# A four-layer graph network on one core: edge sums by feature, two linear layers as one product, and the last layers with the output in groups of 512 nodes

## The reference, cut to what matters

```python
# L3, on nodes v = relu(layernorm(x)); all widths 128 except edge_attr and u (64)
msg = relu(concat(v[src], edge_attr) @ W1a + b1a)
msg = msg @ W1b + b1b
agg = mean of msg over the edges that end in a node (0 where there is none)
out = concat(v, agg, u[0]) @ W2a + b2a
out = relu(out) @ W2b + b2b
return x + out
```

## Time and profile before

| | |
|---|---|
| median of 3 runs | 9359.47 us (9359.37 to 9371.02) |
| profiled execution | span 9364.4 us; no separate device time is given for it, so its span stands 4.9 us above the median |
| TensorE busy | 7028.5 us, 75% |
| VectorE busy | 5660.6 us, 60% |
| ScalarE, GpSimd busy | 2515.7 us, 27%; 2656.2 us, 28% |
| near block of the edge pass | about 8963 to 9216 us of the span |
| the three `dense` calls | 9216.2 to 9350.0 us |
| output transfer | 9350.3 to the end at 9364.4 us |

### The profile page before, as it was taken

The page is one execution under the profiler, slowest core; times in us unless marked ns, Lnnn a source line. Parts: engine busy times, 40 slices in busy tenths (PEclk is TensorE's granted clock), DMA queues, the critical chain, the costliest instruction groups (busy, mean ns, idle before and its releaser), DMA issues. The chain is left out here.

```text
span 9364.4 us, 133857 instructions
## 1 busy us (share of the span) xinstructions
PE 7028.5 (75%) x35740; PEld 4596.9 (49%) x35792; DVE 5660.6 (60%) x16783; ACT 2515.7 (27%) x5863; POOL 2656.2 (28%) x2952
## 2 busy tenths in 40 slices
PE   4777777775566659940488699999998777777787
PEld 4555555453122224420477544444445666666676
DVE  6777777775589990059899800000014777777786
ACT  0222222222467740020388600000001333310001
POOL 0777777776470000000000000000002444444410
PEclk9767776766679989975799899999999999999998
DMA  3333333334975538849566478787886766642363
GB/s 99 103 103 105 105 104 103 105 105 167 393 231 164 168 114 306 299 195 426 205 215 216 144 262 276 262 287 256 295 284 200 181 180 179 179 111 63 63 178 88
DMA packets 969628, 1759.77 MB, mean 188 GB/s; under 512 B 102288, under 2 KB 665125, under 8 KB 905315
## 3 DMA queue, kind: packets, MB, share of 16 engines
q1 hardware_dynamic: 683820, 1335.73, 44.1%
q0 software_dynamic: 110720, 276.01, 9.0%
q10 hardware_dynamic: 174394, 139.51, 5.5%
HBM read 1412.04 MB, written 338.80 MB: 187 GB/s over the span
## 5 line engine op out<-in xcount | busy, mean ns | idle before, releaser
L768 POOL DMA_INDIRECT bucketed<-arena,wide x1563 | 1515.6, 970 | 726.5 <-issue 714.0
L1920 PE MATMUL psum<-wide,arena 128*128 x6496 | 1209.9, 329 | 400.5 <-DVE arena L1979 393.9
L1920 PEld LDWEIGHTS psum<-wide,arena 128*128 128x128 f32 x6496 | 989.9, 195 | 618.3 <-issue 493.3
L1787 POOL DMA_DIRECT2D table<-wide x13 | 9.7, 743 | 4316.2 <-DVE wide L1711 4316.2
L1979 DVE TENSOR_SCALAR arena<-wide,tile_first 128x128 f32 x3248 | 870.8, 300 | 472.3 <-PE psum L1920 293.8
L1841 POOL DMA_INDIRECT arena<-table,src_i x832 | 803.3, 966 | 1009.1 <-PE psum L1937 872.4
L1660 PE MATMUL psum<-arena,h 128*128 128x512 f32 (+1 forms) x2548 | 1048.6, 570 | 19.1 <-DMA arena<-adjacency 17.5
L922 PE MATMUL psum<-arena 128*128 128x512 bf16 x2253 | 695.7, 442 | 435.0 <-DVE arena L870 259.4
L665 PE MATMUL psum<-arena 128*113 128x177 bf16 x1568 | 534.4, 341 | 416.2 <-ACT wide L687 374.6
L870 DVE TENSOR_SCALAR arena<-sums 128x512 bf16<-128x512 int16 x2304 | 799.9, 347 | 0.0
L659 PE MATMUL psum<-w_edge,arena 128*128 128x256 f32 x1568 | 786.9, 597 | 0.0
(11 more groups left out here) (398 smaller groups left out, 11006.0 us busy)
## 6 DMA issues: line engine op xcount, KB each, us to landing
arena<-adjacency SPq DMA_DIRECT2D x294, 1024.0 KB
arena<-adjacency SPq DMA_DIRECT2D x98, 1568.0 KB, 7.8
adjacency<-wide SPq DMA_DIRECT2D x588, 256.0 KB
arena<-adjacency SPq DMA_DIRECT2D x196, 640.0 KB, 3.9
arena<-adjacency SPq DMA_DIRECT2D x147, 768.0 KB
arena<-bucketed POOLq DMA_DIRECT2D x208, 528.0 KB, 6.0
arena<-adjacency SPq DMA_DIRECT2D x49, 1792.0 KB, 6.9
arena<-adjacency SPq DMA_DIRECT2D x49, 1344.0 KB, 6.1
```

The source lines that it names most:

```text
L768: e.indirect_dma_start(bucketed, bass.IndirectOffsetOnAxis(ap=places[k][0:size, c:c + 1], axis=0), rows[k][0:size, c, :], None).then_inc(s ...
L1920: e.matmul(flat[:, ds((chunk & 3) * 512 + 2048, P)], lhsT=hot[:, i % 8, :], rhs=table_in[:, ds(tile * P, P)], start=False, stop=True, skip ...
```

## The change

It does five things.

1. In both blocks of the edge pass the operands of the matmul change places: the messages are now lhsT and the one-hot matrix rhs, so that the 128x128 sum comes out with features on the partitions, and `h` collects sums by feature. The first three lines of work of `dense` (scale, transpose, copy) fall away.
2. W1b @ `W["agg"]` is formed once, before `sage(1)`, by a `run` of nine steps; so are b1b @ `W["agg"]` (`agg_bias`) and the u part of b2a. One product with `w_agg` takes the place of the products with W1b and `W["agg"]`.
3. The node part, v @ `W["h"]` plus `agg_bias` where the node has any edge, is computed in `sage(3)`: 49 more products behind the old ones in `product`, and 49 `scalar_tensor_tensor` on VectorE (`kept_rows`), written over `sums`. `linear` and the passes wait for `kept_rows` now.
4. b2b is added to `x` by one GpSimd instruction over 128x6272 in the near block.
5. `tail()` takes the place of the three `dense` calls, the `run` and `store`: one block in which the 13 groups run through first product, scale and add (VectorE), transpose, bias and ReLU (ScalarE), second product, add to `x`, and each group's own output transfer.

Two of the row vectors loaded at the start become columns, and `dense`'s semaphores go; `gin_mlp` returns its semaphores for use in `tail`.

```diff
-        for name in ("L0_gnn_b1", "L0_gnn_b2", "L0_gnn_gamma", "L0_gnn_beta", "L2_gnn_b1", "L2_gnn_b2"):
+        for name in ("L0_gnn_b1", "L0_gnn_b2", "L0_gnn_gamma", "L0_gnn_beta", "L2_gnn_b1", "L2_gnn_b2", "L3_gnn_b1b", "L3_gnn_b2a"):
             col[name] = sb("c_" + name, [P, 1])
             loads.append((col[name][:, :], t[name].rearrange("(f a) -> f a", a=1)))
...
-                     "L3_gnn_b1a", "L3_gnn_b1b", "L3_gnn_b2a", "L3_gnn_b2b"):
+                     "L3_gnn_b1a", "L3_gnn_b2b"):
...
-        def turn(buffer, k):
...
-        def dense(inputs, finish, reader=0):
...
...
-
-        gin_mlp()
+            return [Baton(signal, GROUPS) for signal in (s_first, s_mid, s_second, s_feat, s_norm, s_turn, s_added)]
+
+        gin_signals = gin_mlp()
...
+        w_agg = W["L3_gnn_W1b"]
+        run([("tensor", lambda e, _: e.transpose(psum[:, 0, 0:P], W["L3_gnn_W1b"][:, :], ident[:, :]), 1),
+             ("vector", lambda e, _: e.tensor_copy(junk[:, :], psum[:, 0, 0:P]), 1),
+             ("tensor", lambda e, _: e.matmul(psum[:, 1, 0:D], lhsT=junk[:, :], rhs=W["agg"][:, :], start=True, stop=True), 1),
+             ("vector", lambda e, _: e.tensor_copy(junk[:, :], col["L3_gnn_b1b"][:, :].broadcast_to([P, P])), 1),
+             ("tensor", lambda e, _: e.matmul(psum[:, 2, 0:D], lhsT=junk[:, :], rhs=W["agg"][:, :], start=True, stop=True), 1),
+             ("tensor", lambda e, _: e.matmul(psum[:, 3, 0:1], lhsT=W["u"][:, :], rhs=u0[:, :], start=True, stop=True), 1),
+             ("vector", lambda e, _: e.tensor_copy(w_agg[:, :], psum[:, 1, 0:D]), 1),
+             ("vector", lambda e, _: e.tensor_copy(agg_bias[:, :], psum[:, 2, 0:D]), 1),
+             ("vector", lambda e, _: e.tensor_tensor(col["L3_gnn_b2a"][:, :], col["L3_gnn_b2a"][:, :], psum[:, 3, 0:1], ALU.add), 1)])
...
-                            e.wait_ge(s_node if more else s_added, g - 1 + (seen if more else 0))
+                            e.wait_ge(s_node if more else s_kept, g - 1 + (seen if more else 0))
...
+                        for c in range(n // P):
+                            last = e.matmul(psum[:, node_bank(p, k), c * P:(c + 1) * P], lhsT=part(wide, a + c * P, P), rhs=W["h"][:, :],
+                                            start=True, stop=True)
+                        last.then_inc(s_root, 1)
...
                                     e.wait_ge(s_row, after[p - 2])
+                                    e.wait_ge(s_kept, after[p - 2])
...
+                    def kept_rows(p, k):
+                        g = PASSES[p][0] + k
+                        a, n = dst_groups[g]
+                        e.wait_ge(s_root, g + 1)
+                        for c in range(n // P):
+                            t = a // P + c
+                            last = e.scalar_tensor_tensor(result[:, t * P:(t + 1) * P], agg_bias[:, :], s["some"][:, t:t + 1],
+                                                          psum[:, node_bank(p, k), c * P:(c + 1) * P], ALU.mult, ALU.add)
+                        last.then_inc(s_kept, 1)
...
                                     table_rows(p, k)
+                                    kept_rows(p, k)
                     if not more:
                         for k in range(PASSES[-1][1]):
                             table_rows(len(PASSES) - 1, k)
+                            kept_rows(len(PASSES) - 1, k)
 
...
-                            last = e.matmul(psum[:, n % 4, 0:D], lhsT=onehot[:, n % 4, c, :], rhs=ring[:, n % DEEP, c, :], start=c == 0, stop=c == PAIR - 1)
+                            last = e.matmul(psum[:, n % 4, 0:P], lhsT=ring[:, n % DEEP, c, :], rhs=onehot[:, n % 4, c, :], start=c == 0, stop=c == PAIR - 1)
...
+                @block.gpsimd
+                def _(e):
+                    e.tensor_tensor(x[:, :, :], x[:, :, :], row["L3_gnn_b2b"][:, :].unsqueeze(1).broadcast_to(tiles()), ALU.add).then_inc(s_biased, 1)
+                    e.wait_ge(s_biased, 1)
...
-                            last = e.matmul(psum[:, n % DEEP, 0:D], lhsT=near_hot[:, n % DEEP, c, :], rhs=near_in[:, g % DEEP, at:at + P],
+                            last = e.matmul(psum[:, n % DEEP, 0:P], lhsT=near_in[:, g % DEEP, at:at + P], rhs=near_hot[:, n % DEEP, c, :],
...
-        dense([(*mean_of_sums(), W["L3_gnn_W1b"])],
-              [("vector", lambda e, i, p: e.tensor_tensor(stage[1][:, :, :], row["L3_gnn_b1b"][:, :].unsqueeze(1).broadcast_to(tiles(BATCH)),
-                                                          s["some"][:, ds(i * BATCH, BATCH)].unsqueeze(2).broadcast_to(tiles(BATCH)), ALU.mult)),
-               ("vector", lambda e, i, p: e.tensor_tensor(batch(wide, i), stage[1][:, :, :], p, ALU.add))], reader=1)
-
-        run([("vector", lambda e, _: e.tensor_copy(junk[0:D_EDGE, :], u0[:, :].broadcast_to([D_EDGE, P])), 1),
-             ("tensor", lambda e, _: e.matmul(flat[:, 0:D], lhsT=junk[0:D_EDGE, :], rhs=W["u"][:, :], start=True, stop=True), 1),
-             ("vector", lambda e, _: e.tensor_tensor(row["L3_gnn_b2a"][:, :], row["L3_gnn_b2a"][:, :], flat[:, 0:D], ALU.add), 1)])
-        dense([(*nodes_of(nodes), W["h"]), ("vector", lambda e, i, out: e.tensor_copy(out[:, :, :], batch(wide, i)), W["agg"])],
-              [("vector", plus_row("L3_gnn_b2a", lambda i: batch(wide2, i))),
-               ("scalar", lambda e, i, p: e.activation(batch(wide2, i), batch(wide2, i), ACT.Relu))])
-        dense([(*nodes_of(wide2), W["L3_gnn_W2b"])],
-              [("vector", plus_row("L3_gnn_b2b", lambda i: batch(wide2, i))),
-               ("vector", lambda e, i, p: e.tensor_tensor(batch(x, i), batch(x, i), batch(wide2, i), ALU.add))])
-        s_out = sem("s_out")
-
-        def store(e, _):
-            e.dma_start(out[0:full_nodes * P, :].rearrange("(i p) f -> p i f", p=P), x[:, 0:full_nodes, :]).then_inc(s_out, 16)
-            e.dma_start(out[full_nodes * P:N_NODES, :], x[0:N_NODES - full_nodes * P, full_nodes, :]).then_inc(s_out, 16)
-            e.wait_ge(s_out, 32)
-            return e.nop()
-        run([("sync", store, 1)])
+        def tail():
+            hidden = [part(arena, 512 * k, 512) for k in range(2)]
+            summed, pre, flipped, hid, product, finished, stored = gin_signals
+            with nc.Block() as block:
+                @block.tensor
+                def _(e):
+                    def first(g):
+                        a, n = dst_groups[g]
+                        if g >= 2:
+                            e.wait_ge(pre.sem, pre.at + g - 1)
+                        for c in range(n // P):
+                            last = e.matmul(psum[:, g % 2, c * P:(c + 1) * P], lhsT=part(h, a + c * P, P), rhs=w_agg[:, :], start=True, stop=True)
+                        last.then_inc(summed.sem, 1)
+
+                    def flip(g):
+                        a, n = dst_groups[g]
+                        e.wait_ge(pre.sem, pre.at + g + 1)
+                        if g >= 2:
+                            e.wait_ge(hid.sem, hid.at + g - 1)
+                        for c in range(n // P):
+                            last = e.transpose(psum[:, 2 + g % 2, c * P:(c + 1) * P], part(sums, a + c * P, P), ident[:, :])
+                        last.then_inc(flipped.sem, 1)
+
+                    def second(g):
+                        a, n = dst_groups[g]
+                        e.wait_ge(hid.sem, hid.at + g + 1)
+                        if g >= 2:
+                            e.wait_ge(finished.sem, finished.at + g - 1)
+                        for c in range(n // P):
+                            last = e.matmul(psum[:, 4 + g % 2, c * P:(c + 1) * P], lhsT=hidden[g % 2][:, c * P:(c + 1) * P], rhs=W["L3_gnn_W2b"][:, :],
+                                            start=True, stop=True)
+                        last.then_inc(product.sem, 1)
+
+                    first(0)
+                    first(1)
+                    for g in range(GROUPS):
+                        flip(g)
+                        if g + 2 < GROUPS:
+                            first(g + 2)
+                        if g:
+                            second(g - 1)
+                    second(GROUPS - 1)
+
+                @block.vector
+                def _(e):
+                    def before_relu(g):
+                        a, n = dst_groups[g]
+                        e.wait_ge(summed.sem, summed.at + g + 1)
+                        for c in range(n // P):
+                            t = a // P + c
+                            last = e.scalar_tensor_tensor(part(sums, t * P, P), psum[:, g % 2, c * P:(c + 1) * P], s["rcount"][:, t:t + 1],
+                                                          part(sums, t * P, P), ALU.mult, ALU.add)
+                        last.then_inc(pre.sem, 1)
+
+                    before_relu(0)
+                    before_relu(1)
+                    for g, (a, n) in enumerate(dst_groups):
+                        if g + 2 < GROUPS:
+                            before_relu(g + 2)
```

(27 more changed lines are left out.)

72 lines of the change are left out of this document (5 added, 67 removed).

## The result

| | before | after |
|---|---|---|
| median of 4 runs each | 9362.70 us (9359.37 to 9371.02) | 9272.53 us (9265.40 to 9279.41) |
| span of the profiled execution | 9364.4 us | 9277.6 us |

The ratio is 0.9899, 95% interval 0.9887 to 0.9911: faster by 90.2 us in the medians, and by 86.8 us between the two profiled spans. Forecast were 9273 us and 9278.5 for the span.

A forecast was written before the change was run, and what follows sets the result against it. TensorE was taken to bound mid-sage(3), TensorE and VectorE the near block, hand-overs the dense calls. Terms -113.4 + 10.7 + 4.8 + 12 = -85.9 us gave a 9278.5 span, 9273 median; range 9257 to 9293.

The forecast's parts named there:

- tail for the `dense` calls and the output: End of the kernel: the new tail takes 35 us in place of 148.2, saving 113 us.
- `sage(3)`, its last three passes and its end: sage(3): 49 added node products lengthen it by 10.7 us (9 to 14).
- run of nine steps: Ahead of sage(1): nine dependent small steps that nothing covers, +4.8 us (3 to 7).
- GpSimd's add against VectorE: Near block: GpSimd's 14.1 us add holds up VectorE's one-hots, about 2 us covered; +12 us (0 to 14).
- operands swapped, loads: Edge matmuls in both blocks and the row loads made column loads: 0 us.
- The period: Tail: TensorE sets the pace at 2.24 us per full group, VectorE needing 1.7 us.
- start at half clock: Tail's beginning: the first 16 product instructions run at 0.22 instead of 0.112 us, costing 1.8 us.
- the clock rival: Tail: clock stays at half, 4.4 us a group, tail 60 us, whole 9298; chance 0.10 for any slower pace.
- Its rival: Tail's output: 13 transfers on one queue delay each other, some 10 of 14.4 us return, 9283; chance 0.06.
- passes 0 and 1: sage(3): products of 32 tiles fall into TensorE's saturated stretch and cost 7.2 us in full.
- pass 2: sage(3)'s last pass: 12 tiles (2.7 us) fall partly into TensorE's adjacency waits; 1.5 us taken, between 0.5 and 2.7.
- the last five tiles: End of sage(3): bare products and kept_rows delay the last table_rows and the next stage by 2 us.

The follow-up runs named there:

- b1: Changed kernel with each waited-for memory value passed through max(value, 0): 9345.46 us.
- b0: Kernel before the change with each waited-for memory value passed through max(value, 0): 9430.63 us.
- c1: b1 without the root product and kept_rows in sage(3), so the output lacks the node part: 9335.81 us.
- r0: Changed kernel with bounds asserted on each register value that a wait reads: 11582.8 us, near block 262.7 us.
- r1: r0 with GpSimd's add of b2b left out: 11575.0 us, near block 252.1 us.
- b3: b1 with the operands of both edge matmuls swapped back: 9345.09 us.
- b2: b1 with b2b added by VectorE in sage(3) instead of GpSimd and the nine-step run moved into sage(1)'s block: 9332.52 us.
- c2: b1 with all output transfers of the tail waiting for the last group: 9357.48 us, tail 44.7 us.
- c3: b1 with the tail's same instructions ordered one group behind the other, without interleaving: 9398.20 us, tail 88.6 us.
- r2: r0 with GpSimd's add replaced by two 128x6272 memsets that nobody reads: 11578.4 us, near block 250.9 us.
- c0: b1 with GpSimd adding b2b group by group in the tail instead of in the near block: 9337.67 us, tail 33.5 us.
- r3: r0 with b2b added by VectorE behind kept_rows in sage(3) instead of by GpSimd: 11559.4 us, near block 252.3 us.

## Why the prediction was right

| term | forecast | between the profiles |
|---|---|---|
| tail for the `dense` calls and the output | -113.4 | -114.7 |
| `sage(3)`, its last three passes and its end | +10.7 | +9.3 (b1 less b0 +9.9, b1 less c1 +9.6) |
| run of nine steps | +4.8 | +4.05 (4.55 in b1) |
| GpSimd's add against VectorE | +12 | +9.6 (r0 less r1 +10.6) |
| operands swapped, loads | 0 | 0 (b3) |
| stages ahead of `sage(1)` | not in the sum | +2.8 |
| `sage(1)`, `sage(2)`, first pass of `sage(3)`, start of the far block | not in the sum | +2.4 |
| what is left | | -0.25 |
| sum | -85.9 | -86.8 |

The two rows "not in the sum" are stretches in which the change alters nothing, and executions of one program differ in them by as much. The last copy before `sage(1)` ended at 5416.4 us in c1 and at 5423.6 in b1, which are the same up to that point, and `sage(1)` with `sage(2)` varied by 4.5 us.

So the mechanisms were right, term by term, but that the sum came out to 0.9 us is in part luck: all four terms that are not nothing were forecast too dear, by 0.75 to 2.4 us and 5.9 together, and 5.2 us from stretches that the forecast rightly left at nothing stand against them in this pair of executions. The median has its own luck. The forecast of 9273 starts from 9359.47 us, and the kernel before measured 9362.70 with the fourth run; the change was forecast at 85.9 us and is 90.2 in the medians.

*The tail.* The period was forecast at 2.24 us and is 2.22; TensorE sets it, as VectorE has 1.81 us (forecast 1.7; four `scalar_tensor_tensor` take 1.12 us with the last one's end, and 8 take 2.16, so one is 0.26 more, as forecast). The term that was mis-sized, and the only one that matters here, is the 1.8 us for a start at half clock. In the profiled execution the first 16 instructions took 2.02 us, at full clock. But the term is no invention: in b2 and c2 the same 16 took 3.29 and 3.57 us, with the clock at 0.60 over b2's first 3.8 us:

```profile
9296.43 3.29 PE L2039 MATMUL psum<-w_L_gnn_W1b,h 128*128 128x128 f32 x16 [1.75 <-PEq L1977]
```

The pause before them is 1.75 us in all of them. The term is paid in some executions, and then costs 1.1 us of the tail (b2: 34.4 for 33.3). The prediction's ground against the clock rival was read too well, though: it says that the clock rose within a few us of dense work. In that call the products still ran at half clock 6 us after the first slow ones, and at full clock 5 us later, with a pause of 1 us before each batch all the while:

```profile
9326.27 3.36 PE L1102 MATMUL psum<-w_L_gnn_W2b,arena 128*128 128x128 f32 x14 [1.00 <-ACT arena L1074]
...
9331.50 1.83 PE L1102 MATMUL psum<-w_L_gnn_W2b,arena 128*128 128x128 f32 x14 [0.99 <-ACT arena L1074]
```

That all groups ran at full clock was no small matter: c3, the same instructions in another order, ran at half clock to its end, so the clock rival (a tail of 60 us) was not far off. What the two traces show side by side is that TensorE is busy 28.0 of 33.5 us with the interleaved order, waiting for 0.33 us at the longest once it has begun, and 60.4 of 88.9 us in c3, waiting for 1.2 and 0.8 us in each period.

*The output.* Its rival fell. One 256 KB transfer per 2.22 us keeps up, and c2 prices the overlap at 10.2 us.

*GpSimd's add.* The mechanism was right: it starts first, and the first one-hot, with both inputs in SBUF, stands still until it ends. The size was off by two parts. The add takes 13.38 us, 2.13 ns an element and not 2.25, so TensorE starts 11.1 us late (13.8 less 2.7); and the block is 10.6 longer in r0 than in r1. What makes up the missing 0.5 was not separated, nor why the block without the add takes 250.9 to 252.3 us in five kernels and 252.8 in the kernel before, which makes the term 9.6 between the profiles. The forecast had 14.1 - 2 = 12. r1, r2 and c0 bound the mechanism: without the add VectorE is not held, with writes alone it is not, and with PSUM as one of its inputs it is not. The Trainium skill, "SBUF — State Buffer", section "Who interferes with whom", says all three: two SBUF inputs contend with a GpSimd instruction that reads SBUF, not with one that only writes it, and one with at most one SBUF input outside the 2-port modes does not contend. By that rule the traces agree, with 13,652 ns for a 416 ns one-hot, 427 at most in r2, and 352 and 689 at most in c0.

*`sage(3)`.* Forecast were 7.2 for passes 0 and 1, 1.5 for pass 2 and 2 for the last five tiles. Measured are 7.15, 1.06 and 1.08 between the profiles, and 7.1, 1.35 and 1.07 between c1 and b1. The first two steps hold: the products of passes 0 and 1 are paid in full, and the 12 tiles of pass 2 fell in part into the waits for the adjacency (2.2 us in the earlier trace rows), as the prediction had it, with 0.5 to 2.7 as bounds. The step that was mis-sized is the end. The last `table_rows` is late by the 2.1 us that were forecast, but not all of that reaches the next block: from its end to the block's first transfer it was 4.7 us and is 3.6 (7160.95 to 7164.58). Before, the two table writes left GpSimd together behind the last `table_rows`, from 7142.29. Now the full group's leaves at 7158.91 and only the small one has to follow, at 7161.24. What one step delayed, the next gave half of back.

*The run of nine steps.* 4.05 us in the profile and 4.55 in b1, for 4.8. In the profile the transpose took 0.30 us and the first product 0.49; I had taken 0.45 and 0.75, and b1 shows 0.45 and 0.79.

*The swap.* 275 ns in both orders, and no change in either block: the near one is 263.3 us for 263.1, and the far one lies at 1862 us inside the 1860 to 1864 of the others with the max.

The median forecast, 9273, is the sum less the 4.9 us by which the profiled span of before stood above its median; the profiled span of after stands 5.1 above its own (9277.6 for 9272.53).

## What to carry to other kernels

That GpSimd is idle in a stage is not enough to give it work: ask from where VectorE reads in that stage. An elementwise add on GpSimd beside two-SBUF-input work on VectorE cost here 10.6 us of its 13.4, where the same add beside work that reads PSUM cost nothing (c0), and on VectorE in a stage with slack 0.6 us (r3), as one of the 13 stood ahead of the last link of that stage's chain. When a chain of small products is cut into groups, write the order so that TensorE has the next group's work during every hand-over: in c3 about half of the price of not doing so was, by estimate, the clock, and no busy time of the other engines would show it. When a stage's length varies by several us between executions of one program, compare the stretch that the edit touches and not the stage: here `sage` hid both what the root product cost in its last pass and what the bias cost at its end. A short setup run that no one needs soon belongs into a block whose first act is to wait for a load (b2).

## What was not expected of the hardware

- The same pause of 1.75 us before the tail is followed by full clock in some executions (2.02 us for 16 instructions) and by half clock in others (3.29, 3.57 us), with the same program behind it but for the edits in b2 and c2.
- In c3 TensorE was busy 60.4 of 88.9 us and had 0.50 of its clock from 2 us on to the end; with interleaved groups it was busy 28.0 of 33.5 and had 1.00.
- GpSimd's add costs 1.27 us for 512 elements a partition and 13.38 for 6272: 2.48 and 2.13 ns each, so a short one pays some 0.18 us more than its share of the long one. A memset of 6272 takes 5.33 us, 0.85 ns each.
